# Projection pieces in two halves over two quarters, and q and k moved forward in the SP queue, in a two-layer transformer kernel

## What is computed

```python
x = _layernorm(x + attention(x, Wq.T, Wk.T, Wv.T, Wo.T, biases, head_mask))   # plain, no mask
h = x + causal_attention(_rmsnorm(x, g1), wq, wk, wv, wo)                      # rotary q and k
y = h + moe(_rmsnorm(h, g2), w_router, wg, wu, wd)                             # top 2 of 8 experts
out = _layernorm(x + y)
```

## Time and profile before

| | us |
|---|---|
| median of 3 runs | 1469.72 (1464.93 to 1469.98) |
| the profiled execution | 1469.85 |
| its span in the trace | 1468.1 |
| first to last exponential of the attention pipeline | 91.37 to 881 |
| PE, DVE, ACT, POOL busy in the whole span | 1280.0, 950.6, 830.1, 796.7 |

### The profile page before, as it was taken

One profiled execution on the slowest core, in us unless ns is written; L12 is line 12 of the kernel. 1 busy time (PEld: TensorE's weight loads), 2 busy tenths in 40 slices (PEclk: granted clock), 3 DMA queues, 4 the chain that ended last, 5 costly groups with the idle time before them and its releaser, 6 DMA issues. The chain is left out here.

```text
span 1468.1 us, 33103 instructions
## 1 busy us (share of the span) xinstructions
PE 1280.0 (87%) x11455; PEld 707.7 (48%) x11456; DVE 950.6 (65%) x1764; ACT 830.1 (57%) x1672; POOL 796.7 (54%) x835
## 2 busy tenths in 40 slices
PE   1799999999989998998999993369999999999990
PEld 0222223232323444444444432358888888888880
DVE  6478888888998787778888721834444444444443
ACT  3148787888888776666676671124444433344334
POOL 2322565475547657566645234146666666666654
PEclk9769999999999999899999895579999999999995
DMA  4416667676767878687867433855232222223326
GB/s 127 87 36 173 178 174 208 187 195 189 186 189 222 218 208 224 201 214 202 209 161 176 115 98 109 255 182 133 45 47 43 43 43 50 43 43 47 45 31 236
DMA packets 159005, 204.45 MB, mean 139 GB/s; under 512 B 31217, under 2 KB 121329, under 8 KB 158897
## 3 DMA queue, kind: packets, MB, share of 16 engines
q1 hardware_dynamic: 141424, 182.55, 45.1%
q0 software_dynamic: 17472, 20.50, 8.8%
HBM read 111.46 MB, written 82.87 MB: 132 GB/s over the span
## 5 line engine op out<-in xcount | busy, mean ns | idle before, releaser
L1006 ACT ACTIVATE a_probs<-a_ps_s 128x512 f32<-128x512 f32 (+2 forms) x896 | 460.4, 569 | 167.1 <-PE a_ps_s L801 161.9
L1075 DVE TENSOR_REDUCE a_shift_max<-a_ps_m 128x1 f16<-128x512 f32 x512 | 320.4, 682 | 70.4 <-PE a_ps_m L806 69.0
L806 PE MATMUL a_ps_m<-a_qkx 48*128 48x128 f16 (+3 forms) x1408 | 286.4, 303 | 18.7 <-DVE a_shift_max L1075 8.9
L1632 PE MATMUL e_ps_gu<-e_xT,w_up 128*128 128x256 f16 x2574 | 298.2, 274 | 1.7 <-ACT e_xT L1686 1.4
L801 PE MATMUL a_ps_s<-a_qkx 49*128 49x128 f16 (+3 forms) x1408 | 277.7, 298 | 14.9 <-ACT a_probs L1006 14.8
L1632 PEld LDWEIGHTS e_ps_gu<-e_xT,w_up 128*128 x2574 | 250.0, 98 | 34.9 <-issue 5.4
L902 PE MATMUL a_ps_o<-a_probs,a_v_one 128*32 128x512 f32 (+3 forms) x2048 | 235.5, 533 | 2.8 <-ACT a_o L1013 2.7
L801 PEld LDWEIGHTS a_ps_s<-a_qkx 49*128 49x128 f16 x1408 | 90.7, 95 | 268.7 <-ACT a_probs L1006 155.8
L1568 POOL DMA_INDIRECT h<-e_y,e_put x78 | 125.5, 1609 | 87.9 <-DVE e_y L1728 67.9
L553 POOL TENSOR_TENSOR a_o_half<-a_o_half,a_inv_half 128x512 f32<-128x512 f32 x32 | 41.1, 1286 | 229.5 <-DMA a_inv_half<-a_inv_dram 229.5
L1740 DVE TENSOR_TENSOR e_h<-e_gate,e_ps_gu 128x512 f32<-128x512 f32 (+2 forms) x156 | 82.6, 550 | 126.0 <-ACT e_gate L1694 107.2
(11 more groups left out here) (194 smaller groups left out, 1662.9 us busy)
## 6 DMA issues: line engine op xcount, KB each, us to landing
a_qkx<-a_qk_dram SPq DMA_DIRECT2D x192, 128.0 KB, 4.3
a_qk_dram<-a_qk SPq DMA_DIRECT2D x32, 512.0 KB, 5.2
a_o_dram<-a_o SPq DMA_DIRECT2D x64, 256.0 KB, 2.9
a_o_half<-a_o_dram SPq DMA_DIRECT2D x32, 256.0 KB
a_inv_half<-a_inv_dram SPq DMA_DIRECT2D x32, 256.0 KB
part<-a_part SPq DMA_DIRECT2D x16, 512.0 KB, 5.7
a_q_swap<-a_q SPq DMA_DIRECT2D x64, 128.0 KB
a_w_in<-in_wg SPq DMA_DIRECT2D x16, 352.0 KB, 5.0
```

The source lines that it names most:

```text
L806: return pe.matmul(out, qx[first:first + 48, r, pair, q * P:(q + 1) * P], kx[first:first + 48, r, pair, k0:k1], start=start, stop=stop)
L1006: act.activation(dst, src, ACT.Exp).then_inc(exp_out, 1)
L1075: vector.tensor_reduce(out, src, AX.X, ALU.max, negate=True).then_inc(max_out, 1)
L1632: mm = pe.matmul(ps_gu[:, bank, kind, f % 2], w[:, ds(e, 1)].rearrange("p o f -> p (o f)"), xT[:, s, xh, k, :], start=n == 0, stop=n == 5)
```

## The change

Heavy pieces are cut in halves: three of the six products of a qk piece, one of the two row tiles of a v or out piece. The piece of quarter 2 is made in quarters 2 and 3, that of quarter 3 in quarters 0 and 1 of the next turn; each is emptied in the quarter of its second half, after the second exponential or maximum (causal: after the first, where a quarter has two). Light pieces are made at the ends of quarters 1 and 3, after `weigh`, and emptied at the start of the next quarter. POOL splits plain q and k after `factors` and `split_x`. In the SP queue the plain q and k are stored in even turns (before `load_o`) and loaded first in odd turns; causal q and k are stored before the weights; the swap stands behind `store_o`.

```diff
-            (1, 0): ("parts", u - 3, 1), (1, 1): ("rows", u, 1), ...
+            (1, 0): ("rows", u, 1), (1, 1): ("parts", u - 3, 1), ...
-            (3, 0): ("parts", u - 2, 0), (3, 1): ("rows", u + 1, 0), ...
+            (3, 0): ("rows", u + 1, 0), (3, 1): ("parts", u - 2, 0), ...
...
-        for i in range(4):
+        for i in (0, 2, 1, 3):
...
                 if n % 2 == 0:
-                    swap((n + 6) // 2)
-                    load_qk((n + 4) // 2)
+                    if causal((n + 4) // 4):
+                        load_qk((n + 4) // 2)
...
                     store_o(n - 1)
+                    swap((n + 6) // 2)
                     for m in weights_at(n - 1):
                         store_weights(m)
                         load_weights(m + 2)
+                    if plain((n + 6) // 4):
+                        store_qk((n + 6) // 2)
                     load_o(n // 2 - 1)
                 else:
+                    if plain((n + 5) // 4):
+                        load_qk((n + 5) // 2)
                     load_rows((n + 1) // 2)
...
                     load_inv((n - 3) // 2)
+                    if causal((n + 5) // 4):
+                        store_qk((n + 5) // 2)
                     for m in weights_at(n - 1):
                         store_weights(m)
                         load_weights(m + 2)
-                    store_qk((n + 5) // 2)
...
                     h = (n + 6) // 2
-                    if plain(h // 2):
-                        split_high(h)
-                        split_low(h)
                     if g == 0:
                         factors(u - 2)
                         split_x(u + 2)
                     else:
                         part_low(u - 2)
+                    if plain(h // 2):
+                        split_high(h)
+                        split_low(h)
                     turn_half(h)
...
+            def half_piece(n, quarter):
+                j = quarter % 2
+                piece = piece_at(n, 2) if quarter >= 2 else piece_at(n - 1, 3)
...
+                if j == 0:
+                    free_piece(piece)
...
+            def light_piece(n, quarter):
+                piece = piece_at(n, quarter // 2) if quarter % 2 else None
...
-                    a_piece(n, quarter)
+                    half_piece(n, quarter)
...
                     else:
                         weigh(n, quarter - 2)
+                    light_piece(n, quarter)
...
-                    early = (1 if quarter < 2 else 0) if causal(u) else 3
+                    early = 0 if causal(u) and quarter >= 2 else 1
+                    empty_light(n, quarter)
...
             def empty_piece(n, quarter):
+                if n % G == 2 and quarter == 3:
+                    residual(n // G - 1, 0)
+                elif n % G == 3 and quarter == 1:
+                    residual(n // G - 1, 1)
```

More of the change, by code:

```diff
@@ L675, in piece_done, with project @@
                 mm.then_inc(piece_mm, 1)
-            def project(u, c):
+            def project(u, c, j):
                 layer = u // B
[L680 to L684, removed]
-                w, m = c % 2, c // 2
-                n = 0
-                for wh, xh in ((0, 0), (0, 1), (1, 0)):
+                if j == 0:
+                    if plain(u):
+                        pe.wait_ge(xT_hi, u + 1)
+                        pe.wait_ge(xT_lo, u + 1)
+                    else:
+                        emptied_piece(pe, "turn", u, 1)
+                w, m = c % 2, c // 2
+                products = [(wh, xh, k) for wh, xh in ((0, 0), (0, 1), (1, 0)) for k in range(KD)]
+                for n in range(3 * j, 3 * j + 3):
+                    wh, xh, k = products[n]
+                    mm = pe.matmul(ps_x[:], t.w_proj[:, 4 * layer + w, wh, k, m * P:(m + 1) * P],
+                                   xT[:, u % 2, xh, k, :], start=n == 0, stop=n == 5)
+                if j == 1:
+                    piece_done(mm, "qk", u, c)
@@ L691, in project @@
                         n += 1
[L692 to L703, removed]
+                if j == 1:
+                    piece_done(mm, "v", u, i)
@@ L723, in turn_maxima, with project_out @@
                 piece_done(mm, "rows", u, c)
-            def project_out(u, i):
+            def project_out(u, i, j):
                 layer = u // B
[L727 to L736, removed]
+                if j == 0:
+                    pe.wait_ge(aT_hi, 2 * u + 2)
+                    pe.wait_ge(aT_lo, 2 * u + 2)
+                n, q = 0, 2 * i + j
+                for wh, ah in ((0, 0), (1, 0), (0, 1)):
+                    for k in range(KD):
+                        mm = pe.matmul(ps_x[:, j * D:(j + 1) * D], aT[:, u % 2, ah, k, q * P:(q + 1) * P],
+                                       t.w_proj[:, 4 * layer + 3, wh, k, :], start=n == 0, stop=n == 5)
+                        n += 1
+                if j == 1:
+                    piece_done(mm, "out", u, i)
             def turn_parts(u, hl):
@@ L963, in move_parts, with empty_piece @@
                 act.activation(nT[:, 0].rearrange("p k s -> p (k s)"), ps_x16[:], ACT.Copy).then_inc(piece_out, 1)
[L965 to L966 removed]
+            def empty_piece(n, quarter):
+                piece = piece_at(n, 2) if quarter == 3 else piece_at(n - 1, 3) if quarter == 1 else None
                 if piece is None:
@@ L973, in empty_piece, with empty_light @@
                     move_v(u, k)
-                elif kind == "rows":
+            def empty_light(n, quarter):
+                piece = piece_at(n, 0) if quarter == 2 else piece_at(n - 1, 1) if quarter == 0 else None
+                if piece is None:
+                    return
+                kind, u, k = piece
+                if kind == "rows":
                     move_rows(u, k)
@@ L1214, in _ @@
                 for quarter in range(4):
-                    early = causal((n + 3) // G)
+                    empty_light(n, quarter)
                     for i in range(4):
@@ L1219, in _ @@
                             causal_row_max(n + 3, quarter, i)
-                        if i == (0 if early else 3):
+                        if i == 1:
                             empty_piece(n, quarter)
```

43 lines of the change are left out of this document (25 added, 18 removed).

## The result

| us | before | after |
|---|---|---|
| median, same comparison | 1469.85 (1464.93 to 1474.81, 4 runs) | 1561.79 (1557.05 to 1563.39, 4 runs) |
| span of the profiled execution | 1468.1 | 1560.5 |
| last exponential of the pipeline ends | 881.7 | 973.1 |

The ratio of after to before is 1.062, with a 95% interval of 1.0577 to 1.0663: 92 us slower, where 12 were predicted. The direction was right and the size wrong by a factor of over seven. The last exponential ends 91.4 us later, and what follows it takes 587.4 us (586.4 before), so all of it was lost in the attention pipeline. Sums of the groups give the plain units +50.2 us (408.8 to 459.0) and the causal ones +42.0 us (381.6 to 423.6). All steps of the prediction are followed in unit 4 here.

The account below looks back on a forecast made before the run. It took plain units as bound by uneven quarters, PE in those with a v piece and ACT or DVE in the others, and causal units by PE. 1469.85 + 11.6 (plain) + 0 (causal) = 1481.5, say 1482 us; range 1454 to 1508.

Parts of the forecast that it names:

- what the halves give: Plain layer: every quarter about 2.87 us of PE, so a unit takes 48.2 us, 2.4 less than 50.6.
- the plain queues: Plain units 2 to 5: late split, denominators, rows and inverses make a unit 53.5 us against 50.6, 11.6 us in all.
- Lands with the 1.5 us that the small store of inverses takes now.: Plain g1, SP queue: after its issue at 25.5 us, the row load lands at 27.0 after g0's start.
- The wait of DVE lying inside that.: Plain g1: DVE's 4 to 5 us wait for denominators adds nothing beyond g2's 3.5 us late start.
- 0, with 5 us either way: Plain units 0, 1, 6 and 7: split 3.2 us earlier, so gain and wait come out even.
- the causal layer: Causal units: 8 us of extra changes to a piece against 7.9 us of removable waits; sum 0, 10 us either way.
- The swap behind `store_o` I cost at nothing: Causal SP queue: the swap's chain ends at 13.9 us, before DVE adds at 14.1, so no cost.
- rival C: Causal odd turns: swap not covered, DVE waits for the sine part, 1.3 us in 16 turns; 1502 us; chance 0.14.
- eight more changes to a piece: Causal PE: extra switches from score tiles to a piece cost about 1 us a unit, 8 us.
- the 7.9 us of waits that could go: Causal PE: 4.2 us for DVE's residual held by POOL and 3.7 us for unloaded q and k could go.
- A: Plain units: halves' gain stands if the split ends before 14.7 us; seven units at -2.4, 1453 us; chance 0.22.
- B: Causal layer: PE isn't the bound, so groups could shorten by 0.8 us in 30 groups; 1458 us; chance 0.14.

Follow-up runs that it names:

- rows_den_first: Changed kernel with denominators and values before the plain q and k store, rows and inverses before the plain load in SP's queue; 1503.46 us, ratio 1.0257.
- all_early: rows_den_first with the swap also moved to just behind the causal q and k load; 1491.79 us, ratio 1.0178 to the kernel before.
- swap_early: Changed kernel with the swap moved to just behind the causal q and k load in SP's queue; 1545.41 us, ratio 1.0538 to the kernel before.

## Why the prediction was right or wrong

**Right in the quarter, too high for most units: what the halves give.** The quarter came to 2.83 us (2.87), and units 0 and 1 of `rows_den_first` last 46.1 and 46.3 us, 3.2 and 3.5 less than before. The cost of a further change to a piece and the ceiling by ACT in g1 (12.1) also hold. But the 48.2 us were for a unit with both POOL steps, and with the queues mended (`all_early`) units 2 to 5 are 49.4 us in the mean: 1.1 less than before and not 2.4. g0 is 12.0 in three of the four (11.4 predicted) and g2 12.3 to 13.4 (11.7); in that run's plain stage PE waits 6.2 us in five waits for POOL's `normalise`.

**Right in mechanism, mis-sized: the plain queues.** Units 2 to 5 lost 37.3 us together and not 11.6. The split, the store and the denominators came within 0.4 us of their predicted times, and DVE's wait (4.09 us) was in its range. Three terms failed:

- "Lands with the 1.5 us that the small store of inverses takes now." That row was taken where no load of q and k stood before it; here 768 KB do, the small store took 6.5 us, and the rows came at 31.6 and not 27.0. The rule of the Trainium skill cited above had been put beside the step as one that "only strengthens" it, with a price of up to 3 us a half; it should have been in the sum. PE waited 20.3 us for rows in the plain stage.
- "The wait of DVE lying inside that." PE's lead hid 1.3 us of DVE's 4.09 (1.8 predicted), so PE stood 2.76. But that wait with the slow stretch behind it brought PE to g2's first score at 345.29, 29.8 us after g0's start: later than the 27.0 at which the rows were to set the start. Even with the rows on time g2 would have begun late.
- No term at all for the clock. PE's busy time rose by 17.6 us in the plain stage. That is about a third of the 49 us that this stage became longer; it is the granted clock's doing as far as the windows can tell, since in `all_early`, with the same halves and no such waits, PE's busy time is 380.43 us at a clock of 1.00. In the causal stage the clock's share of the 15.4 us isn't separated: `all_early` has 9.5 us more than before there, at 0.95 against 0.96.

The output projection's wait was over-stated: PE waited 4.2 us in four waits for POOL's part, about 1 us each and not 1.8. And units 0, 1, 6 and 7, taken as "0, with 5 us either way", came out as -1.5, +6.9, +4.2 and +3.3, together +12.9: the small DMAs stand behind the large ones there too. The bounds (1464 to 1508) left these 5 us out and took 8 of the causal layer's 10 at the upper end; with both the upper end is 1515, still far from 1561.79.

**Wrong: the causal layer.** The sum was 0 and the result +42. The step that failed first is "The swap behind `store_o` I cost at nothing", with 1.8 us of issues and 3 of landing; 9.1 us passed from the first issue to the multiply. That is rival C, with the sign and the wait that it named (DVE waits 18.4 us in nine waits for the sine part in the whole causal stage), but its 20 us is only half of the loss. Mending the swap's place gave some 12 us, alone and on top of the other repairs; in the profiles 7 to 9 of them are in the causal units. The rest, 30 us in `all_early`, stands where "eight more changes to a piece" at "about 1 us a unit" had 8: with one bank for all pieces, a rows piece that follows directly on an output piece's second half waits for the residual, and PE's waits for the bank rose from 10 to 30 us. Of the 7.9 us of waits that could go one grew: the wait for the residual was 15.0 us in the changed kernel. That the residual "comes a quarter later" was put down as a gain, and what comes after it in the bank was left out. That this order is the cause of the 30 us is read from the waits; no run moved the light pieces alone.

**The other rivals.** A (the gain stands) failed where it said it would be decided: the split ends at 18.4 us, not before 14.7. Its gain is there in part once the order is mended, 12 us in the plain stage where it said 17. B (PE isn't the causal bound) found nothing: no run with halves in the causal layer has a shorter causal stage, and g0, the group that was gapless, grew from 11.6 to 12.7 us. The Trainium skill's advice to judge TensorE's headroom by its weight loads' busy share and not by that of its matmuls (Perfetto Trace Analysis, section Identifying the Most-Contended Engine) would have promised room, at 6.01 us of 11.63; none of these runs found any in a stage in which the products follow each other without a gap.

**What stays open.** How the causal loss divides among halves, the places of light pieces and SP's causal order; why `swap_early` still has g3 at 14 to 18 us although DVE waits only 7.0 us for the sine part there; why the plain g2 with mended queues is longer than 11.7 us; and what the clock would have been with the same waits but another mix of work.

## What to carry to other kernels

When a DMA is moved in an in-order queue, ask two things of each step behind it: when the moved one's own wait is met, and how many bytes then stand in front of a small transfer that somebody waits for; the landing time of that small transfer in its old place is no price for the new one. Cutting work in halves evens out an engine that has gaps; in the stage that had none it gained nothing here, and with it the order of the neighbours in the one shared buffer became part of the change. And a wait of TensorE in a full pipeline should be costed with what comes after it as well: here a third of the loss was busy time, not idle time.

## What the runs showed of the hardware

A granted clock of 0.50 (1.2 of 2.4 GHz) isn't a thing of a kernel's start alone. The kernel before has it inside its attention pipeline too (586.7 to 596.9 us). In that of after it was seen around waits of TensorE, as in the one of 4.22 us that ended at 821.61, and stayed for up to 10.2 us (819.20 to 829.40), in which three products of 512 columns took 1.46 us and not 0.82. And a 16 KB store needed 6.5 us to be told as landed behind 768 KB of loads, against 1.5 to 2.6 without them.
